# First layer of a two-layer graph network: work of GpSimd moved to VectorE, masks in one-input form, picks at set steps

## The chip, the cores and the metric

The kernel runs on one core of a Trainium2 chip. The core has TensorE (PE in the profile), VectorE (DVE), ScalarE (ACT), GpSimd (POOL) and SyncE (SP), 16 DMA engines, an SBUF of 128 partitions and a PSUM of eight banks. The metric is the device time of one execution in microseconds, lower is better. The kernel before has a median of 3579.48 us over three runs, from 3570.99 to 3601.28.

## The reference

There are 6250 nodes with 128 features, 200,000 edges sorted by destination, eight edge types and four node types.

```python
# first layer
neigh_sum = jax.ops.segment_sum(x[src], dst, num_segments=N)
deg = jax.ops.segment_sum(jnp.ones_like(src, dtype=x.dtype), dst, num_segments=N)
mean = neigh_sum / jnp.maximum(deg, 1.0)[:, None]
neigh_agg = jnp.where(deg[:, None] > 0, mean, x)
h = relu(jnp.concatenate([x, neigh_agg], axis=-1) @ W.T + b)
x1 = layernorm(x + h)
# second layer: attention over the edges
Q, K, V = (type_matmul(x1, W, node_type) for W in (W_Q, W_K, W_V))
k_t = type_matmul(K[src], W_edge, edge_type)
scores = jnp.sum(Q[dst] * k_t, axis=-1) / sqrt(d) * mu[edge_type]
out = segment_sum(V[src] * segment_softmax(scores, dst)[:, None], dst)
y = layernorm(x1 + out)
```

## The kernel before

**Stages.** Setup loads the edges, tests that they are sorted densely enough for the quick form (the other form is a loop that here runs once), and splits x into a bfloat16 part and two rests, x_parts, that sum to it with little loss. The first layer's loop, `l0`, has 49 iterations (ND = TILES = 49). The second layer then works through 98 blocks of 2048 edges and gathers a row of keys and values per edge from `kv_table`.

**The loop of the first layer.** Edges are laid in columns of 128. A period of 32 columns goes through one iteration, in two ways. The first 14 columns, in two halves of HALF = 7, are gathered: GpSimd issues one indirect DMA per column (line 717), which fetches 128 rows of `part_dram` into one of three run buffers `near` (two in the ring, the third over `src_n`). TensorE multiplies each with a mask that says to which node an edge belongs (`belongs`, made by VectorE on line 1414) and sums seven in PSUM: the run product, `run_sum`, line 803, at steps 2 and 23. GpSimd may refill a run buffer once the run product of that buffer is counted in `runs_ps`. The other 18 columns (GCOLS) are done without a gather. For each, VectorE writes two one-hot masks (`hot`, lines 1382 and 1383, six batches of three columns into a ring of nine), TensorE multiplies them (a pick, line 769, into one of two banks), and ScalarE copies the result to SBUF (`take`, line 1138). A pick needs the copy of the pick two before it. With all 18 picks of an iteration copied, the next iteration's 49 slot sums (line 777), one per step h from 0 to 48, multiply them with all of x_parts.

**The tail of a tile** runs inside the same iterations: at iteration i the tile i-2 is `early` (mean, transposes, first product, `relu`, `normalise_x1`) and tile i-3 is `late` (transpose of the normalised rows, `by_types`, key and value projections, `low_keys` and `high_keys`, copies into `kv_rows`). SP stores the rows of x1, the typed rows and the 1 MB table row block of each tile, and loads the next x and types.

**The order is written out by hand.** TensorE's order and its waits are a list of steps h in `l0` of the tensor block: `PICK_AT` gives the steps of the picks, and `HOT_AT`, one step before every third pick, the waits for masks. ScalarE's order is its list of copies c from 0 to 17 with the tile's copies between them. VectorE has its own `l0`: it joins the slot sums of the iteration before, makes masks, adds node sums, does the tile's steps and then stages the keys of the iteration after next (line 1375). In iterations 4 to 12 a digit pass over all 1664 columns comes first (`digit_op`, nine passes; SP stores the result before tile 12). GpSimd's program is the gathers, with two pieces of arithmetic between the first groups: `edge_keys` (three passes over 128x1664, lines 699 to 703) before group 2 and `weights` (eight scalings, line 694) before group 3.

## Time and profile before

| What | Value |
|---|---|
| Median of three runs | 3579.48 us (3570.99 to 3601.28) |
| The profiled execution's own time | 3594.51 us |
| Its span, first to last instruction | 3592.7 us, 38408 instructions |
| Mean granted TensorE clock | 0.839 of full |
| TensorE matmul, busy | 2618.7 us, 73%, 13802 instructions |
| VectorE, busy | 1554.8 us, 43%, 4730 instructions |
| ScalarE, busy | 1151.8 us, 32%, 2057 instructions |
| GpSimd, busy | 2244.9 us, 62%, 2302 instructions |
| Chain that ended last, by engine | GpSimd 36%, TensorE 25%, issue 18%, another core or an unknown queue 13%, VectorE 5% |
| First layer's gathers, line 717 | 462 into the ring at 1028 ns, 224 into src_n at 1038 ns |

The shares are means over both layers, which have different limits. Busy time is from the first to the last record of an instruction; matmuls overlap and their ends are modelled. "Remote" or "another core or an unknown queue" is what the profile says of a wait whose releaser it does not see at that time; this kernel has one core. The granted clock is 1.0 at 2.4 GHz and 0.5 at 1.2 GHz.

### The profile page before, as it was taken

The numbers are of one execution on the slowest core, as the hardware profiler recorded it, in microseconds if no ns is written. First come the engines' busy times: TensorE is split into PE (matmuls) and PEld (weight loads), VectorE is DVE, ScalarE is ACT, GpSimd is POOL, SyncE is SP. The second block draws the span as 40 slices with busy tenths as digits, with TensorE's granted clock in tenths as the row PEclk, the third lists the DMA queues.
The fourth block names the chain that finished last, engine by engine and source line by source line (L and its number), as shares of the span: only waits on it lengthen the run. The fifth ranks groups of instructions, "written<-read, shape, count | busy, mean of one in ns | idle before, by whom it ended". The sixth has DMA issues, their size and how long they took to land.

```text
span 3592.7 us, 38408 instructions
## 1 busy us (share of the span) xinstructions
PE 2618.7 (73%) x13802; PEld 1868.6 (52%) x13802; DVE 1554.8 (43%) x4730; ACT 1151.8 (32%) x2057; POOL 2244.9 (62%) x2302
## 2 busy tenths in 40 slices
PE   3587888887878827777777777777777777777777
PEld 1355566555556625555554555555555555555555
DVE  8476677666667613322322233322322333323223
ACT  4344454444444412222222222222222222222222
POOL 7665566566556454666666666666666666666664
PEclk9799999899999968777778887777777877777778
DMA  6244354444444432333333333333333333333332
GB/s 157 62 129 121 111 144 130 120 126 120 119 119 126 118 122 75 100 99 100 100 100 101 103 100 100 99 97 100 100 100 102 102 100 101 100 99 100 101 100 69
DMA packets 256960, 384.03 MB, mean 107 GB/s; under 512 B 100640, under 2 KB 189003, under 8 KB 250625
## 3 DMA queue, kind: packets, MB, share of 16 engines
q0 software_dynamic: 108112, 273.13, 27.6%
q1 hardware_dynamic: 146833, 107.53, 9.7%
q8 instruction: 108, 1.77, 0.2%
q10 hardware_dynamic: 1824, 0.92, 0.1%
q14 instruction: 83, 0.68, 0.1%
HBM read 304.30 MB, written 77.13 MB: 106 GB/s over the span
## 4 chain that ended last, share of the span: by engine, by line
POOL 36%; PE 25%; issue 18%; another core or an unknown queue 13%; DVE 5%; ACT 2%; DMA 0%; ACTq 0%; DVEq 0%; POOLq 0%
POOL ring L722 35%; PE banks L777 9%; PE banks L769 4%; PE banks L803 3%; PE banks L850 1%; PE banks L862 1%; PE banks L992 1%; PE banks L855 1%; PE banks L1005 1%; ACT picks L1138 1%; PE banks L1029 1%; PE banks L865 1%; PE banks L1021 1%; POOL ring L717 1%
## 5 line engine op out<-in xcount | busy, mean ns | idle before, releaser
L722 POOL DMA_INDIRECT ring<-kv_table,src_n x1563 | 1485.4, 950 | 798.3 <-issue 447.6
L1005 PE MATMUL banks<-identf,ring 128*128 128x128 f32 x1568 | 436.9, 373 | 630.4 <-issue 501.1
L717 POOL DMA_INDIRECT ring<-x_part_rows,work x462 | 475.1, 1028 | 307.4 <-PE banks L803 142.8
L1005 PEld LDWEIGHTS banks<-identf,ring 128*128 128x128 f32 x1568 | 250.9, 182 | 791.1 <-issue 585.2
L777 PE MATMUL banks<-sums,picks 128*126 128x385 bf16 x2401 | 608.1, 342 | 33.3 <-ACT picks L1138 15.3
L1138 ACT ACTIVATE picks<-banks 128x343 bf16<-128x343 f32 x882 | 433.3, 512 | 543.7 <-PE banks L769 333.6
L1227 ACT ACTIVATE work<-banks 128x512 f32<-128x512 f32 x392 | 213.5, 598 | 887.6 <-remote 638.9
L1623 DVE SCALAR_TENSOR_TENSOR sums<-sums,corr,banks 128x128 f32<-128x128 f32 x98 | 34.0, 347 | 1029.2 <-remote 1022.6
L1219 ACT ACTIVATE work<-banks,negmax 128x2048 f32<-128x2048 f32 x98 | 192.8, 1968 | 807.9 <-issue 743.7
L777 PEld LDWEIGHTS banks<-sums,picks 128*126 128x126 bf16 x2401 | 331.6, 143 | 149.4 <-issue 54.1
L769 PE MATMUL banks<-sums 128*128 128x343 bf16 x882 | 286.1, 325 | 168.7 <-issue 105.8
L1604 DVE TENSOR_REDUCE largest<-banks 128x1 f32<-128x2048 f32 x98 | 224.5, 2291 | 370.5 <-PE banks L992 273.6
L1029 PE MATMUL banks<-ring,sums 128*128 128x128 f32 x3136 | 372.7, 277 | 5.6 <-issue 4.5
L992 PE MATMUL banks<-work,queries 128*128 128x512 f32 x784 | 372.8, 619 | 0.0
L1029 PEld LDWEIGHTS banks<-ring,sums 128*128 128x128 f32 x3136 | 358.6, 192 | 6.5 <-issue 5.1
L1661 DVE COPY sums<-banks 128x512 f32<-128x512 f32 x392 | 262.5, 689 | 148.6 <-PE banks L1021 101.7
L717 POOL DMA_INDIRECT src_n<-x_part_rows,work x224 | 232.5, 1038 | 136.6 <-issue 60.5
L1021 PE MATMUL banks<-identf,work 128*128 128x128 f32 x1568 | 313.0, 384 | 1.1 <-ACT work L1219 1.1
L1021 PEld LDWEIGHTS banks<-identf,work 128*128 128x128 f32 x1568 | 303.0, 212 | 2.4 <-ACT work L1219 1.3
L1383 DVE TENSOR_SCALAR sums<-iota_k,keys_g 128x344 bf16<-128x344 bf16 x882 | 288.4, 327 | 0.0
L1382 DVE TENSOR_SCALAR sums<-iota_n,keys_g 128x128 bf16<-128x128 bf16 x882 | 238.7, 271 | 114.3 <-PE banks L769 58.9
L992 PEld LDWEIGHTS banks<-work,queries 128*128 128x128 f32 x784 | 144.7, 195 | 189.7 <-issue 189.7
(260 smaller groups left out, 2363.3 us busy)
## 6 DMA issues: line engine op xcount, KB each, us to landing
kv_table<-ring SPq DMA_DIRECT2D x48, 1024.0 KB
ring<-kv_table,src_n POOLq DMA_INDIRECT x1563
sums<-x_typed SPq DMA_DIRECT2D x99, 128.0 KB
x_typed<-work SPq DMA_DIRECT2D x49, 256.0 KB
ring<-x_part_rows,work POOLq DMA_INDIRECT x462
x_part_rows<-sums SPq DMA_DIRECT2D x7, 675.5 KB, 7.1
src_n<-x_part_rows,work POOLq DMA_INDIRECT x224
sums<-x_rows SPq DMA_DIRECT2D x51, 64.0 KB
```

What stands on the lines that cost most here:

```text
L717: pool.indirect_dma_start(near[k % RUNS][:, j, :], None, part_dram, bass.IndirectOffsetOnAxis(ap=col_ids[:, first + j:first + j + 1], axis ...
L722: pool.indirect_dma_start(kv_ring[u][:, j, :], None, table, bass.IndirectOffsetOnAxis(ap=of, axis=0)).then_inc(l1_rows[2 * u + j // RUN], 16)
L769: pe.matmul(bank[c % 2][:, 0:KEYS], hot_low[:, c % HOT_RING, :], hot_key[:, c % HOT_RING, 0:KEYS], start=True, stop=True).then_inc(pick_ps, 1)
L777: mm = pe.matmul(bank[2 + i % 2][0:SLOTS, 0:3 * D + 1], picked[:, i % 2, h, 0:SLOTS], x_parts[:, h, 0:3 * D + 1], start=(h == 0), stop=(h ...
L992: mm = pe.matmul(bank[g], queries[:, :], keysT[:, g, :], start=False, stop=True, skip_group_check=True)
L1005: tr = pe.transpose(bank[KEY_BANK[g]][:, j * P:(j + 1) * P], kv_ring[k.u][:, g * 4 + j, 0:D], identf[:, :])
L1021: tr = pe.transpose(bank[PROB_BANK[g]][:, j * P:(j + 1) * P], probT[:, at:at + P], identf[:, :])
L1029: mm = pe.matmul(bank[7][:, 0:D], prob[:, j, :], kv_ring[k.u][:, j, D:2 * D], start=(j == 0), stop=(j == COLS - 1))
L1138: act.activation(picked[:, par, :, c * NW:(c + 1) * NW], bank[c % 2][:, 0:KEYS].rearrange("p (h w) -> p h w", w=NW), ACT.Copy).then_inc(pi ...
L1382: dve.tensor_scalar(hot_low[:, c % HOT_RING, :], iota_n[:, :], keys_g[:, par, 1, c:c + 1], None, ALU.is_equal)
L1383: ins = dve.tensor_scalar(hot_key[:, c % HOT_RING, :], iota_k[:, :], keys_g[:, par, 0, c:c + 1], None, ALU.is_equal)
L1661: dve.tensor_copy(prob[:, g * 4:(g + 1) * 4, :].rearrange("p a b -> p (a b)"), bank[PROB_BANK[g]]).then_inc(prob_copied, 1)
```

## The change

GpSimd keeps only its gathers. `weights` and `edge_keys` become VectorE's: the weights in iteration 0, the keys as four pieces of one two-input operation each in iterations 1 and 2. The third run buffer moves from `src_n` to `spare_n`, since `src_n` must live until the keys are made and then serves as the digits' scratch. The digits are made in thirds of the columns, 27 short passes in iterations 4 to 30, no longer ahead of everything; SP's store of them moves from before tile 12 to before tile 30. A run mask is made by seven one-input operations on a bfloat16 `iota_g` rather than by one two-input fp32 operation. `PICK_AT` is a written list, the wait for the first batch of hot masks moves from step 48 to step 2 of the next iteration, and four of ScalarE's copies move by one or two places. VectorE's order within an iteration changes, and the row normalisation of a tile is done at the head of the next iteration.

```diff
-        iota_g = sb("iota_g", [P, P])
+        iota_g = sb("iota_g", [P, P], BF16)
...
-        near_runs = [near_flat[:, 0:HALF * TW // 2], near_flat[:, HALF * TW // 2:], src_n[:, 0:HALF * TW // 2].bitcast(F32)]
+        near_runs = [near_flat[:, 0:HALF * TW // 2], near_flat[:, HALF * TW // 2:], spare_n[:, 0:HALF * TW // 2].bitcast(F32)]
...
+        DIGIT_COLS = [k * CBLKS // 3 * P for k in range(4)]
+        DIGIT_ALL = 3 * DIGIT_OPS
         DIGIT_STEP = 4
+        KEY_OPS = 4
+        KEY_COLS = [k * NAT // KEY_OPS for k in range(KEY_OPS + 1)]
...
-                if t == 12:
-                    sp.wait_ge(digit_vec, DIGIT_OPS)
+                if t == 30:
+                    sp.wait_ge(digit_vec, DIGIT_ALL)
                     store_digits()
...
             for k in range(2 * ND):
-                if k == RUNS - 1:
-                    edge_keys()
-                    pool.wait_ge(keys_nat, 1)
-                if k == RUNS:
-                    weights()
                 if k >= RUNS:
                     pool.wait_ge(runs_ps, k - RUNS + 1)
...
-            PICK_AT = [-(-c * TILES // GCOLS) for c in range(GCOLS)]
+            PICK_AT = [3, 4, 7, 10, 14, 17, 18, 19, 22, 24, 25, 28, 29, 31, 33, 37, 42, 44]
...
-                    if i + 2 < ND and h == TILES - 1:
-                        wait_hot(i + 2, 0)
+                    if 0 < i < ND - 1 and h == 2:
+                        wait_hot(i + 1, 0)
                     slot_sum(i, h)
...
-                    if late and c == 11:
+                    if late and c == 12:
                         copy_high(late)
-                    if early and c == 11:
+                    if early and c == 13:
                         copy_x(early)
-                    if early and c == 13:
+                    if early and c == 14:
                         copy_mean(early)
-                    if early and c == 16:
+                    if early and c == GCOLS - 1:
                         deviation(early)
...
-                dve.tensor_tensor(belongs[h], col_keys[:, 1, first:first + HALF].unsqueeze(2).broadcast_to([P, HALF, P]),
-                                  iota_g[:, :].unsqueeze(1).broadcast_to([P, HALF, P]), ALU.is_equal).then_inc(belongs_ready, 1)
+                for j in range(HALF):
+                    ins = dve.tensor_scalar(belongs[h][:, j, :], iota_g[:, :], col_keys[:, 1, first + j:first + j + 1], None,
+                                            ALU.is_equal)
+                ins.then_inc(belongs_ready, 1)
...
+            def edge_keys(k):
+                at = slice(KEY_COLS[k], KEY_COLS[k + 1])
+                if k == 0:
+                    dve.wait_ge(L["etype"], 48)
+                dve.scalar_tensor_tensor(key_f[:, at], src_n[:, at], float(ET), et_n[:, at], ALU.mult, ALU.add
+                                         ).then_inc(keys_nat, 1)
...
             def l0(i, late, early):
-                if DIGIT_STEP <= i < DIGIT_STEP + DIGIT_OPS:
-                    digit_op(i - DIGIT_STEP)
                 if i > 0:
                     join_parts(i - 1, (i - 1) % 2)
+                if late:
+                    normalise_x1(late)
                 if i + 1 < ND:
                     hot(i + 1, (i + 1) % 2, 2)
-                    belong(i + 1, 0)
                 if i > 0:
                     add_nodes(i - 1)
                 if late:
                     by_types(late)
+                if i + 1 < ND:
+                    hot(i + 1, (i + 1) % 2, 3)
                 if early:
                     mean(early, added(i))
                 if i + 1 < ND:
-                    for q in range(3, BATCHES):
+                    for q in range(4, BATCHES):
                         hot(i + 1, (i + 1) % 2, q)
+                    belong(i + 1, 0)
+                if i == 0:
+                    weights()
+                if 1 <= i <= KEY_OPS // 2:
+                    for k in range(2 * i - 2, 2 * i):
+                        edge_keys(k)
+                if DIGIT_STEP <= i < DIGIT_STEP + DIGIT_ALL:
+                    digit_op(i - DIGIT_STEP)
                 if late:
                     copy_low(late)
                 add_runs(i)
...
-                if early:
+                if i == ND - 1:
                     normalise_x1(early)
```

## Rows read from the trace of the kernel before

**Rows 1.** Windows by stage: length, busy us and count by engine, clock, DMA share, GB/s.

```profile
...
72.60:190.80 118.20, 73.55 (x370) 47.84 (x368) 63.45 (x217) 40.37 (x83) 78.43 (x77) 0.83 0.26 68
190.80:1231.40 1040.60, 861.35 (x4927) 605.79 (x4927) 728.99 (x2860) 483.56 (x1056) 630.91 (x611) 0.94 0.44 124
...
1275.60:3592.70 2317.10, 1633.81 (x8264) 1181.13 (x8264) 680.29 (x1446) 578.11 (x843) 1486.36 (x1564) 0.79 0.35 98
```

**Rows 2.** One line's instructions in the loop: ns, first and last start.

```profile
L1375 DVE COPY keys_g<-work x44: 168/174/179, 187.1 to 1205.3; 128x36 f32<-128x36 f32 x44
```

**Rows 3.** Windows of a fast and a slow iteration, columns as in rows 1.

```profile
498.60:519.70 21.10, 18.55 (x115) 13.24 (x113) 16.63 (x67) 10.86 (x25) 14.72 (x15) 1.00 0.49 139
...
701.70:729.60 27.90, 21.99 (x117) 15.80 (x118) 16.34 (x67) 12.27 (x29) 13.24 (x14) 0.81 0.36 107
```

**Rows 4.** Timeline, fast iteration, TensorE: start, us, count, idle before and releaser.

```profile
511.16 1.32 PE L803 MATMUL banks<-src_n,more_belongs 128*128 128x385 bf16 x7
...
516.68 0.32 PE L769 MATMUL banks<-sums 128*128 128x343 bf16 x1 [1.91 <-issue]
```

**Rows 5.** Timelines of ScalarE, VectorE and GpSimd at the same place.

```profile
516.12 1.42 ACT L1138 ACTIVATE picks<-banks 128x343 bf16<-128x343 f32 x3 [3.31 <-remote]
...
516.18 0.69 DVE L1478 COPY ring<-banks 128x512 f32<-128x512 f32 x1 [2.97 <-remote]
...
513.96 0.95 POOL L717 DMA_INDIRECT ring<-x_part_rows,work  x1 [0.31 <-issue]
516.31 0.95 POOL L717 DMA_INDIRECT src_n<-x_part_rows,work  x1 [1.41 <-remote]
```

**Rows 6.** Waits in the loop: us in total, times, longest.

```profile
ACT picks L1138 <- remote: 144.6, 51, 4.6
```

**Rows 7.** Timelines of VectorE's masks and of the gathers that run beside them.

```profile
497.35 1.09 DVE L1414 TENSOR_TENSOR more_belongs<-work,iota_g 128x896 bf16<-128x896 f32 x1
...
499.29 0.24 DVE L1382 TENSOR_SCALAR sums<-iota_n,keys_g 128x128 bf16<-128x128 bf16 x1
499.44 0.30 DVE L1383 TENSOR_SCALAR sums<-iota_k,keys_g 128x344 bf16<-128x344 bf16 x1
...
505.42 1.09 DVE L1414 TENSOR_TENSOR ring<-work,iota_g 128x896 bf16<-128x896 f32 x1 [0.22 <-remote]
...
497.77 1.49 POOL L717 DMA_INDIRECT ring<-x_part_rows,work  x1 [0.30 <-issue]
499.57 0.99 POOL L717 DMA_INDIRECT ring<-x_part_rows,work  x1 [0.30 <-issue]
...
505.65 1.67 POOL L717 DMA_INDIRECT ring<-x_part_rows,work  x1 [1.32 <-remote]
```

**Rows 8.** Timeline of GpSimd at the start.

```profile
77.53 4.44 POOL L699 TENSOR_SCALAR spare_n<-src_n 128x1664 int32<-128x1664 int32 x1
...
87.73 1.05 POOL L717 DMA_INDIRECT src_n<-x_part_rows,work  x1 [0.28 <-POOL et_n L703]
...
97.06 3.64 POOL L694 TENSOR_SCALAR ring<-ring,mu_b 128x128 f32<-128x128 f32 x8
100.97 1.01 POOL L717 DMA_INDIRECT ring<-x_part_rows,work  x1 [0.27 <-issue]
```

**Rows 9.** Timeline of TensorE at the start: two run products.

```profile
98.71 2.43 PE L803 MATMUL banks<-src_n,ring 128*128 128x385 bf16 x7 [2.87 <-DMA src_n<-x_part_rows,work]
...
111.33 2.18 PE L803 MATMUL banks<-ring,more_belongs 128*128 128x385 bf16 x7 [4.94 <-DMA ring<-x_part_rows,work]
```

**Rows 10.** VectorE groups, 190 to 420 us: busy us, mean ns, idle before.

```profile
L1493 DVE SCALAR_TENSOR_TENSOR digits<-digits 128x1664 bf16<-128x1664 bf16 x1 | 1.9, 1883 | 0.0
```

**Rows 11.** Groups in the loop, shapes kept apart, columns as in rows 10.

```profile
L777 PE MATMUL banks<-sums,picks 128*126 128x385 bf16 x2158 | 547.1, 341 | 26.9 <-ACT picks L1138 13.7 <-issue 10.9 <-DVE ring L1405 2.0
```

**Rows 12.** Timeline of TensorE across an iteration's boundary.

```profile
660.36 0.32 PE L769 MATMUL banks<-sums 128*128 128x343 bf16 x1 [2.23 <-ACT picks L1138]
661.73 0.90 PE L777 MATMUL banks<-sums,picks 128*126 128x385 bf16 x2 [1.04 <-ACT picks L1138]
```

More of the change, by code:

```diff
@@ L689, in _ @@
                                         ).then_inc(gen_loaded, 16)
-            def weights():
-                pool.wait_ge(L["small"], 16)
-                pool.wait_ge(L["weights"], 80)
-                for e in range(ET):
-                    pool.tensor_scalar(we_s[:, e, :], we_s[:, e, :], mu_b[:, e:e + 1], SCALE, ALU.mult, ALU.mult
-                                       ).then_inc(weights_ready, 1)
-            def edge_keys():
-                pool.wait_ge(L["etype"], 48)
-                pool.tensor_scalar(spare_n[:, :], src_n[:, :], float(ET), None, ALU.mult).then_inc(pool_step, 1)
-                pool.wait_ge(pool_step, 2)
-                pool.tensor_tensor(et_n[:, :], spare_n[:, :], et_n[:, :], ALU.add).then_inc(pool_step, 1)
-                pool.wait_ge(pool_step, 3)
-                pool.tensor_copy(key_f, et_n[:, :]).then_inc(keys_nat, 1)
             pool.wait_ge(parts_stored, 16 * (TILES // 7))
@@ L967, in _ @@
             late_part(tile(TILES - 1))
-            pe.wait_ge(keys_nat, 1)
+            pe.wait_ge(keys_nat, KEY_OPS)
             pe.wait_ge(picked_ready, ND * GCOLS + 2)
@@ L1478, in copy_low, with weights, digit_op @@
                 dve.tensor_copy(kv_of(tile)[:, 0:4, 0:D], by_type(bank[6])).then_inc(kw_low, 1)
-            def digit_op(k):
-                dve.wait_ge(*((digit_vec, k) if k else (keys_nat, 1)))
-                X, Y, Z = (digits[:, i, :] for i in range(3))
-                if k == 0:
-                    ins = dve.tensor_scalar(spare_n[:, :], dst_n[:, :], 3, 15, ALU.arith_shift_right, ALU.bitwise_and)
+            def weights():
+                dve.wait_ge(L["small"], 16)
+                dve.wait_ge(L["weights"], 80)
+                for e in range(ET):
+                    dve.tensor_scalar(we_s[:, e, :], we_s[:, e, :], mu_b[:, e:e + 1], SCALE, ALU.mult, ALU.mult
+                                      ).then_inc(weights_ready, 1)
+            def edge_keys(k):
+                at = slice(KEY_COLS[k], KEY_COLS[k + 1])
+                if k == 0:
+                    dve.wait_ge(L["etype"], 48)
+                dve.scalar_tensor_tensor(key_f[:, at], src_n[:, at], float(ET), et_n[:, at], ALU.mult, ALU.add
+                                         ).then_inc(keys_nat, 1)
+            def digit_op(n):
+                dve.wait_ge(*((digit_vec, n) if n else (keys_nat, KEY_OPS)))
+                part, k = divmod(n, DIGIT_OPS)
+                at = slice(DIGIT_COLS[part], DIGIT_COLS[part + 1])
+                X, Y, Z = (digits[:, i, at] for i in range(3))
+                near_dst, spare_d = dst_n[:, at], src_n[:, at]
+                half = half_b[:, at]
+                if k == 0:
+                    ins = dve.tensor_scalar(spare_d, near_dst, 3, 15, ALU.arith_shift_right, ALU.bitwise_and)
                 elif k == 1:
-                    ins = dve.tensor_scalar(X, spare_n[:, :], -2.0, 16.0, ALU.mult, ALU.add)
+                    ins = dve.tensor_scalar(X, spare_d, -2.0, 16.0, ALU.mult, ALU.add)
                 elif k == 2:
-                    ins = dve.tensor_scalar(spare_n[:, :], dst_n[:, :], 7, None, ALU.bitwise_and)
+                    ins = dve.tensor_scalar(spare_d, near_dst, 7, None, ALU.bitwise_and)
                 elif k == 3:
-                    ins = dve.tensor_scalar(Y, spare_n[:, :], -2.0, 8.0, ALU.mult, ALU.add)
+                    ins = dve.tensor_scalar(Y, spare_d, -2.0, 8.0, ALU.mult, ALU.add)
                 elif k == 4:
@@ L1494, in digit_op @@
                 elif k == 5:
[L1495 removed]
+                    ins = dve.scalar_tensor_tensor(half, Y, 0.25, Y, ALU.mult, ALU.mult)
                 elif k == 7:
[L1497 removed]
+                    ins = dve.tensor_scalar(half, near_dst, 0.0, FAR_PLACE, ALU.is_lt, ALU.mult)
                 else:
[L1499 removed]
+                    ins = dve.tensor_tensor(Z, Z, half, ALU.add)
                 ins.then_inc(digit_vec, 1)
             def l0(i, late, early):
[L1503 to L1504 removed]
                 if i > 0:
                     join_parts(i - 1, (i - 1) % 2)
+                if late:
+                    normalise_x1(late)
                 if i + 1 < ND:
                     hot(i + 1, (i + 1) % 2, 2)
[L1509 removed]
                 if i > 0:
```

6 lines of the change are left out of this document (1 added, 5 removed).

## The prediction

> **What bounds the kernel now.** I first cut the span into stages [rows 1]. The second layer is the largest, 2317.1 us from 1275.6 us on. No line of it is edited, and its inputs are the same, so I carry it over unchanged. The first layer's loop runs at a settled pace from 190.8 to 1231.4 us. There TensorE is busy for 861.35 of 1040.6 us, at a mean granted clock of 0.94. Before it lies a start of 118.2 us with TensorE busy for only 73.55. So the change can act on some 1160 us. In the loop the keys are staged once per iteration, 44 times from 187.1 to 1205.3 us [rows 2]: 1018.2 / 43 = 23.7 us an iteration. Two iterations show the ends of the spread [rows 3]: one takes 21.1 us with TensorE busy for 18.55 at full clock, the other 27.9 us at a clock of 0.81.
>
> From these rows the mean iteration splits into three. TensorE's work at full clock is 18.5 us. The clock costs 1.4: at 0.94 with levels of 1.0 and 0.5, 12% of 1040.6 us is spent at 1.2 GHz, 125 us, of which half is lost, 62 us over 44 iterations. TensorE's idle time is (1040.6 - 861.35) / 44 = 4.1 us. Together that is 24.0, close to 23.7.
>
> What sets the 21.1 is the reading that matters most. TensorE's run product at 511.16 us has all its operands and its last matmul ends at 512.5; TensorE goes on, then stops and begins its next pick only at 516.68, 1.91 us idle [rows 4]. In between, ScalarE, VectorE and GpSimd are all waiting for counts that only TensorE raises, and start within 0.2 us of each other: 516.12, 516.18 and 516.31 [rows 5]. GpSimd's last gather of the group of seven before that ended at 513.96 + 0.95 = 514.91. So TensorE's counts arrive about 1.2 us after the gather group in progress ends, although its matmuls were over 3.6 us earlier. I do not know why, but it ties TensorE to GpSimd: the page calls such a releaser "remote", and ScalarE alone lost 144.6 us to it in 51 waits [rows 6]. A cycle of the fast iteration is therefore two gather groups with their gaps: from 505.65 to 516.31 us is 10.66 us, and two such make the 21.1. GpSimd, through this, is the bound of a fast iteration. TensorE is the bound of a slow one, where GpSimd waits for it.
>
> **The change, part by part.**
>
> *Run masks.* Each group's mask is one two-input fp32 operation of 1.09 us. Two gathers that begin beside one take 1.49 and 1.67 us, while one beside the one-input hot masks takes 0.99, and one beside nothing 0.95 [rows 7, 5]. Two masks per iteration so cost GpSimd 0.54 + 0.72 = 1.26 us of the 21.1. The new form is seven one-input masks of the shape of the hot mask on line 1382. Two such masks start 0.15 us apart or a little more [rows 7], so seven are about 1.1 us and VectorE's time stays as it is. Upper bound: seven at 0.25, 1.75 us, also hidden, since VectorE is busy for 16.6 of 21.1 us [rows 3]. What they do to a gather lies between nothing and the old 1.26; nearest is the row beside hot masks, +0.04 per gather, so some 0.15 us per iteration comes back. Gain 1.1 us in an iteration bound by GpSimd, nothing in the others. By the two ends of rows 3, the mean of 23.7 makes (27.9 - 23.7) / 6.8, 60%, fast ones; I take half, 22. **-24 us**, bounds 0 and -48.
> The Trainium skill ("SBUF — State Buffer", section "SBUF: two separate sides") says that VectorE and GpSimd share a port pair as an exclusive lock, which a 2-port fast mode takes always and a two-input operation only against a GpSimd operation that reads SBUF. By that rule the new masks, in a fast mode, would block as the old ones do, and the sum would be 24 us worse. The trace shows the two-input form hurting and the fast form (0.04 us) hardly at all.
>
> *GpSimd's own arithmetic.* Edge keys held its gathers from 77.53 to 87.73, 10.2 us, the weights from 97.06 to 100.97, 3.9 us [rows 8]. TensorE then waited 2.87 and 4.94 us for two gathered groups [rows 9]. Gain: at least those 7.8, at most all 14.1 us. I take **-10**, as the waits on held counts that follow are not removed. What moves to VectorE: eight weight scalings, which cost GpSimd 3.64 us and so VectorE hardly more; four key pieces (one pass rather than three, each over a quarter of the columns); all in iterations 0 to 2, where VectorE is busy for 63.45 of 118.2 us [rows 1]. That idle time covers them. Without it, some 6 us: 3.64 and about one pass of 1.88 [rows 10]. The third run buffer moves to another tile, which costs nothing. The digit stores stay on SP's queue but go behind tile 30 rather than 12: six issues that wait for nothing by then, needed first after the loop.
>
> *Digits in thirds.* Nine passes of 1.0 to 1.9 us (the largest row 1.88 [rows 10]) stood ahead of everything in VectorE's iterations 4 to 12, so ahead of masks TensorE needs. Now 27 passes of a third stand behind the masks. Between nothing and nine times 1.9, 17 us; near the middle, **-8**. The added fixed costs, 18 instructions of about 0.1 us, are hidden on VectorE.
>
> *Picks by time.* The last pick was at step 47 of 49, and TensorE's first slot sum of the next iteration waits for ScalarE's copy of it. The idle time before slot sums is 26.9 us in the loop [rows 11]; now the last pick is at step 44, and this goes. The wait for the first hot masks of the iteration after next, at step 48, moves to step 2 of the next; an iteration boundary shows 2.23 us before a pick and 1.04 before the slot sum [rows 12]. If ten boundaries have the 2.23, that is 22 more. In a fast iteration the held counts take the time back, so half: **-25**, bounds 0 and -49. Against it: the picks after the second run product now stand at steps 24, 25 and 28, not 25, 28 and 30. A pick needs the copy of the one two before it, and that copy waits for the held count, so TensorE stops two steps earlier. A step is one matmul, at most 0.19 us by the seven in 1.32 [rows 4]: at most 0.38 x 44 = +17, and at least 0. I take **+5**, as in a fast iteration GpSimd sets the pace.
>
> *Deferred normalisation* takes VectorE's wait for ScalarE's square root off the end of an iteration. It puts the row normalisation behind the join of the slot sums, still ahead of step 9 where TensorE transposes it. SP's store and reload of x wait for it about 1 us longer, with nobody waiting for them. Node sums and row types now come ahead of the run mask: the old mask waited for the run product just before them. Both: 0, bounds +-5.
>
> *The clock.* If TensorE idles less it falls to 1.2 GHz less often; of the 62 us I take a tenth, **-6**, bounds +20 and -30.
>
> Sum: -24 - 10 - 8 - 25 + 5 - 6 = -68 us against the profiled execution's 3594.5, so 3526.5. That execution lay 15.0 us above the median of 3579.5, so the forecast is **3511 us**.
>
> **The rivals.**
>
> *Hidden anyway (0.22).* TensorE's held counts and its clock set the pace whatever the masks do; the mean of 23.7 against the fast 21.1 speaks for it, the 1.49 and 1.67 against. Only the start and the digits count: 3579.5 - 10 = about 3569.
>
> *The masks still lock GpSimd (0.13).* The seven fast masks follow each other without a gap, other than the pairs in rows 7, and the gather beside them is blocked for all of their 1.1 us. The 24 us stay away: 3535. This is the skill's lock rule as a mechanism of this kernel.
>
> *Picks run into the held counts (0.12), slower.* The place is steps 3 to 7 and 24 to 28. The first pick now stands right behind the first run product, and the pick at step 7 needs its copy. Between that run product and step 7 lie five slot sums, two picks (0.19 each, 1.3 us) and four small node products, some 1.8 us; if the count is held longer than this, TensorE stops there too, about 0.5 us, and 0.3 at step 28. With the idle time the clock falls more often, so some 1.0 us for 44 iterations is +44, and less 10 for the start: about 3615. For it: each hold lasts 3.6 us in rows 4. Against it: with shorter gather groups holds end sooner.
>
> *All iterations become fast (0.08).* At 21.1 - 1.1 = 20.0 us each, 44 take 880 of 1040.6 us: -160, and -10: 3409, with the clock's share perhaps 3430.
>
> **How the numbers follow.** The forecast has 0.45, the likeliest case, and 3511 is its time. The range takes in the forecast's bounds as far as they are not all on one side, the case of locked masks, and the hidden case with its spread: 3435 to 3578. What it leaves out is the slower rival and most of the fast one, under 0.2. About 1% (36 us) is what a measurement can tell from no change. Faster by more: 0.45 + 0.13 + 0.08 = 0.66; within: 0.22; slower: 0.12.
>
> **What would show it.** Masks: gathers beside the new masks take about 1.0 us and none 1.5; the fast iterations last 20.0. Start: no GpSimd arithmetic, and the run products at 98.71 and 111.33 come 3 and 8 us earlier. Picks: the idle time before slot sums falls from 26.9 us to near 5. Digits: iterations 4 to 12 no longer than the rest. The forecast is wrong if the staging of keys still comes every 23.7 us, or if TensorE's idle time of 179 us only moves to the picks at steps 7 and 28; if the second layer moves by over 10 us, the cause lies outside my steps.

## The result and the profile after

The changed kernel has a median of 3607.85 us (3595.10 to 3623.57, eight runs), the kernel before, timed beside it, 3574.06 us (3551.95 to 3601.28, eight runs). The ratio is 1.0084 with an interval of 1.0045 to 1.0124. All ratios here leave out the slow runs of either kernel (over 1.5% above its fastest, among them single ones of 6683 and 4587 us). I had forecast 3511 us; the change makes the kernel slower by a little. The profiled execution took 3607.77 us, with a span of 3606.0.

Three words are used from here on. A count is the increment of a semaphore that TensorE makes when a matmul ends and for which another engine waits. A count is held when it is recorded well after the end of its matmul. A group is the seven gathers that fill one run buffer.

The stages come first, in windows with the columns of [rows 1]: the loop (from the first slot sum of iteration 4 to that of iteration 48), and the rest.

```profile
186.80:1242.30 1055.50, 846.08 (x4929) 585.48 (x4930) 745.09 (x3410) 472.03 (x1056) 593.41 (x609) 0.98 0.43 122
1242.30:3606.00 2363.70, 1671.47 (x8451) 1212.07 (x8450) 703.97 (x1530) 590.06 (x869) 1500.37 (x1566) 0.78 0.35 99
```

In the kernel before the loop is 190.8 to 1231.4 [rows 1], and the rest:

```profile
1231.40:3592.70 2361.30, 1666.77 (x8450) 1205.35 (x8450) 701.95 (x1528) 589.57 (x868) 1487.50 (x1566) 0.79 0.35 99
```

The 13.3 us between the spans are -4.0 in the start, +14.9 in the loop and +2.4 behind it. The -4.0 is no gain that can be told from chance: e9 and e10 below run the changed kernel's program up to iteration 24, and their start ends at 187.5 and 173.9 us. In the loop GpSimd's busy time falls from 630.91 us [rows 1] to 593.41, as forecast: no gather of 609 takes over 1.3 us, where it was 63 of 611. TensorE's clock rises from 0.94 to 0.98. Yet an iteration takes 24.0 us and not 23.65, for TensorE's idle time grew by 30.2 us (1055.50 - 846.08 = 209.4, before 179.2) and its busy time fell by only 15.3. Where it idles, by line and by waits in the loop:

```profile
L760 PE MATMUL banks<-sums,picks 128*126 128x385 bf16 x2157 | 545.6, 331 | 73.2 <-ACT picks L1121 71.5 <-issue 1.7
```

```profile
ACT picks L1121 <- remote: 231.6, 72, 5.1
POOL ring L700 <- PE banks L786: 193.0, 57, 5.7
...
POOL spare_n L700 <- PE banks L786: 91.4, 26, 5.4
```

The idle time before slot sums, which was to fall from 26.9 [rows 11] to near 5 us, is 73.2. ScalarE's waits for held counts ("remote") went from 144.6 us [rows 6] to 231.6. GpSimd waits 284.4 us for run products; the same two rows of the kernel before add to 184.0:

```profile
POOL ring L717 <- PE banks L803: 124.5, 29, 9.8
...
POOL src_n L717 <- PE banks L803: 59.5, 15, 10.0
```

Timelines of one turn show the pattern, TensorE, GpSimd and ScalarE:

```profile
506.06 0.32 PE L752 MATMUL banks<-sums 128*128 128x343 bf16 x1 [2.49 <-issue]
507.58 2.42 PE L786 MATMUL banks<-spare_n,more_belongs 128*128 128x385 bf16 x7
```

```profile
497.55 0.95 POOL L700 DMA_INDIRECT ring<-x_part_rows,work  x1 [3.98 <-PE banks L786]
...
505.17 0.96 POOL L700 DMA_INDIRECT ring<-x_part_rows,work  x1 [0.30 <-issue]
510.27 1.24 POOL L700 DMA_INDIRECT spare_n<-x_part_rows,work  x1 [4.14 <-PE banks L786]
```

```profile
505.39 0.61 ACT L1121 ACTIVATE picks<-banks 128x343 bf16<-128x343 f32 x1 [4.32 <-remote]
```

The group of gathers ends at 506.13. ScalarE has waited 4.32 us for the count of a pick made long before, TensorE stops 2.49 us for ScalarE's copy, and only then, behind the pick, comes the run product at 507.58 that lets GpSimd go on, 4.14 us idle. In the fast iteration of before, the stop at 516.68 stood behind the run product at 511.16 [rows 4], and GpSimd lost 1.41 us [rows 5]. The clock has fallen as well: the granted clock is 1.00 from 500 to 506 us and 0.53 from 507.5 to 510, so this product takes 2.42 us and not 1.32. In the changed loop TensorE stops at the pick of step 19 for 74.7 us in 39 iterations, and at the slot sum of step 0 for 73.2 us in 41: both ahead of a run product (steps 23 and 2).

### The profile page after: what moved, and what is told of

The parts are those of the page before. It is cut to its first block, busy times and chain, and to the rows that moved or that the text cites. A ratio compares the mean times of both kernels' runs of the same rounds, so it can differ in the third digit from the quotient of the medians.

```text
span 3606.0 us, 39015 instructions
## 1 busy us (share of the span) xinstructions
PE 2609.4 (72%) x13802; PEld 1853.7 (51%) x13802; DVE 1569.0 (44%) x5348; ACT 1138.9 (32%) x2057; POOL 2207.2 (61%) x2291
## 4 chain that ended last, share of the span: by engine, by line
POOL 40%; PE 25%; issue 17%; another core or an unknown queue 13%; ACT 4%; DVE 2%; DMA 0%; ACTq 0%; DVEq 0%; POOLq 0%
POOL ring L705 40%; PE banks L760 9%; PE banks L752 6%; ACT picks L1121 2%; PE banks L786 2%; PE banks L833 1%; PE banks L845 1%; PE banks L838 1%; PE banks L848 1%; ACT ring L1143 1%; PE banks L775 1%; PE banks L975 1%; PE banks L805 0%; PE banks L1004 0%
## 5 line engine op out<-in xcount | busy, mean ns | idle before, releaser
L988 PE MATMUL banks<-identf,ring 128*128 128x128 f32 x1568 | 414.7, 367 | 632.8 <-issue 400.0
L700 POOL DMA_INDIRECT ring<-x_part_rows,work x462 | 451.8, 978 | 342.0 <-PE banks L786 209.4
L975 PE MATMUL banks<-work,queries 128*128 128x512 f32 x784 | 387.6, 640 | 0.0
L700 POOL DMA_INDIRECT spare_n<-x_part_rows,work x224 | 218.0, 973 | 163.2 <-PE banks L786 99.3
L1365 DVE TENSOR_SCALAR sums<-iota_n,keys_g 128x128 bf16<-128x128 bf16 x882 | 230.7, 262 | 193.8 <-remote 106.9
L1366 DVE TENSOR_SCALAR sums<-iota_k,keys_g 128x344 bf16<-128x344 bf16 x882 | 280.6, 318 | 0.1
```

What stands on the lines that cost most here:

```text
L700: pool.indirect_dma_start(near[k % RUNS][:, j, :], None, part_dram, bass.IndirectOffsetOnAxis(ap=col_ids[:, first + j:first + j + 1], axis ...
L975: mm = pe.matmul(bank[g], queries[:, :], keysT[:, g, :], start=False, stop=True, skip_group_check=True)
L988: tr = pe.transpose(bank[KEY_BANK[g]][:, j * P:(j + 1) * P], kv_ring[k.u][:, g * 4 + j, 0:D], identf[:, :])
L1365: dve.tensor_scalar(hot_low[:, c % HOT_RING, :], iota_n[:, :], keys_g[:, par, 1, c:c + 1], None, ALU.is_equal)
L1366: ins = dve.tensor_scalar(hot_key[:, c % HOT_RING, :], iota_k[:, :], keys_g[:, par, 0, c:c + 1], None, ALU.is_equal)
```

## The experiments

The table takes each loop from the same two slot sums: us per iteration, TensorE's idle time in the 44 iterations, its mean clock, and held counts: those of TensorE's counts in the loop that arrive over 0.8 us after their matmul's end, of all that the records let me match. Of the 1320 that a loop raises 15 to 31% have no record or no match, and with another way of matching the first two rows are 221 of 1073 and 266 of 1038 and the two brakes 13 and 5: the column tells some 250 from some 20, no more.

The runs came in series, each with the kernel before timed beside it, and ratios are against that. Its medians were 3644 us (e1 to e4), 3646 (e5 to e8), 3570 (e9 to e12), 3013 (e13 to e16) and 3579 (e17, e18). The other columns come from one profiled execution each, and the first two rows' from the first series of all (3574 us). They carry the difference between series with them: the rest behind the loop, the same work in every kernel, takes 2361 to 2364 us in the first two profiles and 2376 to 2382 in those of e1 to e8. So compare a ratio with a ratio, and across series with caution.

| Kernel | ratio, interval | iteration | idle | clock | held |
|---|---|---|---|---|---|
| before | 1 | 23.65 | 179 | 0.94 | 250 of 1126 |
| changed | 1.0084 (1.0045-1.0124) | 23.99 | 209 | 0.98 | 312 of 1072 |
| e1 changed, old picks | 1.0386 (1.0284-1.0488) | 27.19 | 259 | 0.88 | 243 of 977 |
| e2 before, new picks | 0.9886 (0.9827-0.9945) | 23.35 | 170 | 0.98 | 274 of 1005 |
| e3 changed, old masks | 1.0151 (1.0024-1.0277) | 24.96 | 214 | 0.92 | 239 of 1032 |
| e4 before, new masks | 1.0459 (1.0355-1.0564) | 27.85 | 282 | 0.87 | 237 of 937 |
| e5 before, both | 1.0339 (1.0292-1.0386) | 27.24 | 291 | 0.93 | 281 of 908 |
| e6 e2 and start, digits | 0.9895 (0.9823-0.9968) | 23.93 | 182 | 0.95 | 258 of 997 |
| e8 products earlier | 1.0132 (1.0076-1.0188) | 25.42 | 223 | 0.90 | 275 of 991 |
| e11 changed, brake | 1.0200 (1.0144-1.0257) | 25.16 | 224 | 0.91 | 22 of 1019 |
| e12 e5, brake | 1.0236 (1.0164-1.0308) | 25.37 | 232 | 0.91 | 7 of 1036 |
| e17 e4, memset | 1.0413 (1.0371-1.0454) | 26.45 | 246 | 0.90 | 260 of 1009 |
| e18 changed, memset | 1.0053 (1.0025-1.0080) | 23.76 | 204 | 0.98 | 309 of 1082 |

**e1 and e2: the picks.** The edit, in e2 forwards and in e1 back:

```diff
-            PICK_AT = [-(-c * TILES // GCOLS) for c in range(GCOLS)]
+            PICK_AT = [3, 4, 7, 10, 14, 17, 18, 19, 22, 24, 25, 28, 29, 31, 33, 37, 42, 44]
```

with the wait for hot masks and ScalarE's order of copies.

> The changed kernel with the pick steps, the wait for the first hot masks and ScalarE's copy order of the kernel before; all the rest of the change stays. Held-count theory: TensorE's counts raised late in a gather group arrive 1.0 to 1.5 us after the group's end. In the changed kernel the pick at step 19 and the slot sum at step 0 stand before the next run product and wait for such a count, so groups and products take turns: 24.0 us an iteration. With the old steps the stalled picks stand behind the run products again, and with the shorter groups an iteration falls to 20 to 22 us: 80 to 150 us faster than the changed kernel, below the kernel before. Rival, VectorE's order: the deferred normalisation and the late run masks make TensorE wait; then the time stays within 15 us of the changed kernel's 3608.

> The kernel before with the changed kernel's pick steps, wait for the first hot masks and ScalarE copy order alone. Held-count theory: the pattern of the changed kernel appears: idle time at steps 19 and 0, few falls of the clock, and with the longer groups (9.1 to 9.3 us rather than 8.8) an iteration of 24.3 to 24.8 us, so 25 to 50 us slower than the kernel before, with the start unchanged. Rival, VectorE's order: the time stays at the kernel before's 3574 within 15 us or falls, since only VectorE's order cost time.

The held-count theory is flatly wrong in both: without the new picks the changed kernel is 3% slower still, and alone they make the kernel before 1.1% faster. e2's rival, which puts the loss on VectorE's order, had the time right. The loss is not in the picks.

**e3 and e4: the run masks.**

```diff
-                dve.tensor_tensor(belongs[h], ...broadcast_to([P, HALF, P]), ALU.is_equal).then_inc(belongs_ready, 1)
+                for j in range(HALF):
+                    ins = dve.tensor_scalar(belongs[h][:, j, :], iota_g[:, :], col_keys[...], None, ALU.is_equal)
+                ins.then_inc(belongs_ready, 1)
```

> The changed kernel with the run mask as one two-input fp32 operation again, on the same places. Held-count theory: in the changed kernel GpSimd's group lies on the cycle twice per iteration, so the masks' lock of GpSimd costs its 0.5 to 0.7 us wherever the mask runs beside a gather: up to 1.2 us an iteration, 20 to 50 us slower than the changed kernel. Rival, the masks do not matter: within 10 us of it; if the masks in one-input form are themselves the loss, faster than it.

> The kernel before with the one-input run masks alone. Held-count theory and my forecast's term: gathers lose their 1.49 and 1.67 us cases, groups take 8.6 us rather than 9.1 to 9.3, the fast iterations go from 21.1 to 20.0 us, and the time falls by 24 to 48 us. Rival, the clock takes it back: TensorE's margin in a fast iteration shrinks, falls to 1.2 GHz become as frequent or more, and the time stays within 10 us.

e3 does not show the gain that taking the masks out should have brought if they alone were the loss: 1.0151 beside 1.0084, with intervals that overlap. In the changed kernel the new masks cost nothing that can be told. In the kernel before they do: alone they make it 4.6% slower where e4's expectation was 24 to 48 us faster, though the median gather is 0.95 us and one of 609 takes over 1.3. Waits of e4's loop, then its timelines of TensorE and GpSimd:

```profile
PE banks L769 <- ACT picks L1138: 187.9, 89, 4.4
...
PE banks L777 <- DVE ring L1405: 0.4, 1, 0.4
```

```profile
POOL ring L717 <- PE banks L803: 324.9, 58, 6.9
POOL src_n L717 <- PE banks L803: 137.5, 25, 6.9
```

```profile
704.33 0.32 PE L769 MATMUL banks<-sums 128*128 128x343 bf16 x1 [2.93 <-issue]
...
704.65 2.22 PE L803 MATMUL banks<-ring,more_belongs 128*128 128x385 bf16 x7
```

```profile
707.14 0.94 POOL L717 DMA_INDIRECT ring<-x_part_rows,work  x1 [3.66 <-PE banks L803]
```

TensorE stops at the pick of step 22 (146.5 us in 41 iterations), which stands ahead of the run product of step 23. The granted clock is 1.00 from 700 to 704.3 us and 0.56 from 704.6 to 707, so the product takes 2.22 us instead of 1.32 [rows 4], and GpSimd waits for all of it, 462.4 us in the loop where it was 184.0. Shorter groups became longer waits for the next. It is not VectorE's time: 0.4 us of TensorE's idle time in this loop ends with VectorE, 223 us with ScalarE's copies.

**e5 and e6: together, and the rest.**

> Before with the one-input run masks, and with the new places of the picks (and their wait for hot masks and ScalarE's order of copies). Alone the masks made before 4.6% slower and the picks made it 1.1% faster. If the two are independent it comes out 3.5% above before. Theory of the phase (what the short gather groups cost is decided by whether a held pick stands just ahead of a run product; the picks' places decide that): the masks' loss mostly goes away, within 1% of before, iterations of 23.5 to 24 us. Rival (the masks cost VectorE or GpSimd time of their own whatever the picks do): 2.5% or more above before, iterations of 26 us.

> Before with the new picks, and with the start and digits of the change: GpSimd only gathers, VectorE scales the weights and makes the edge keys, digits in thirds at the head of VectorE's iterations. Two-input run masks and VectorE's other order as before. If these parts are worth what I forecast (10 us at the start, 8 for the digits), it lies 0.5% below before with new picks alone, so 1.6% below before. Rival, where the loss between that kernel and the changed one with old masks (2.6%) comes from these parts: 1% or more above before, and then VectorE's order and the deferred normalisation are innocent; if it stays at -1.1 to -1.6%, the loss is in VectorE's order or the deferral.

The masks cost 4.6% with the new picks too (1.0339 / 0.9886), so with VectorE's old order the two are independent, and e5's theory of the phase is wrong. The start and the digits are worth nothing (0.9895 against 0.9886). What is left of the change is VectorE's order and the deferred normalisation. It makes the kernel 2.6% slower with the old masks (e6 to e3) and 2.5% faster with the new ones (e5 to changed). It has no price of its own. Both steps compare across series. Inside one series, with the start and the digits taken in, it is 2.7% slower by the ratios from e2 to e3 (1.9% by the means of their runs) and 0.7% faster from e4 to e1, both of these with the new masks (3788 to 3801 and 3765 to 3773 us). So the loss beside the old masks is firm, and the gain beside the new ones is there, but its size is not.

**e7: no gathers** in iterations 25 to 48.

```diff
-                for j in range(HALF):
+                for j in range(HALF if k < 50 else 0):
```

> The changed kernel, with the gathers of its groups 50 to 97 left out (iterations 25 to 48): the run products of those iterations take stale rows at once. GpSimd only passes its waits there. One trace shows the loop with and without gathers. Theory (TensorE's counts are held because GpSimd is issuing gathers): from iteration 25 on no count lags by over 0.1 us, TensorE's idle time at picks and slot sums goes, the clock stays at full speed, and an iteration takes 18.5 to 20 us against 24 before it. Rival (the held counts are TensorE's own affair, or that of its clock or of ScalarE and VectorE): lags and stalls stay, an iteration takes 22.5 us or more.

Its windows, one inside the part with gathers and one without:

```profile
184.40:666.00 481.60, 377.57 (x2028) 258.90 (x2029) 311.88 (x1423) 194.26 (x433) 246.33 (x253) 0.90 0.38 109
730.00:1142.00 412.00, 412.00 (x2593) 309.98 (x2591) 372.16 (x1781) 248.05 (x556) 0.00 (x0) 1.00 0.26 90
```

Without them each iteration takes 17.8 us (26.5 with them in this run, iterations 4 to 23), TensorE is never idle and no count is held. The holds come with the gathers, and both together cost 8.7 us an iteration here. The 26.5 is a warning too: up to iteration 24 this is the changed kernel, whose own profile has 23.9 us in the same iterations, so against that the cost is 6.1 us. e7, e9 and e10 are one execution each.

**e8: run products at steps 0 and 17.**

```diff
-            RUN_AT = (2, 23)
+            RUN_AT = (0, 17)
```

> The changed kernel with its run products moved ahead of the two places where TensorE stalls most: from steps 2 and 23 to steps 0 and 17, each before the pick and the slot sum of that step (the waits for run sums and masks move to step 48 and 16). The stalls stood at the pick of step 19 (74.7 us) and the slot sum of step 0 (73.2 us), and GpSimd idled 3.7 to 4.1 us ahead of each group for the product behind them. Theory of the phase: GpSimd starts its groups earlier and works while TensorE is stalled instead of after it, so its idle time before a group falls by 2 us or more and an iteration goes from 24.0 to 22.5 us or less: 60 us, 1.7% faster than the changed kernel. Rival (a group of gathers holds the counts wherever it lies, so an earlier group only stalls the picks elsewhere): within 0.7% of the changed kernel, with the stalls at other steps.

Wrong again: an iteration takes 25.4 us, not 22.5 or less. TensorE:

```profile
707.56 1.32 PE L786 MATMUL banks<-ring,more_belongs 128*128 128x385 bf16 x7
...
713.85 0.32 PE L752 MATMUL banks<-sums 128*128 128x343 bf16 x1 [3.47 <-ACT picks L1119]
```

The product's own count is held too, 4.3 us, and comes at 713.13, 0.16 us after the last gather of the group in progress has landed (GpSimd starts its next at 713.39), and the uneven halves of 17 and 32 steps leave GpSimd idle in the long one. Its waits for run products are 286.3 us in this loop, no less than the 284.4 of the changed kernel.

**e9 and e10: bytes.** Half rows, and a second 1 MB store per tile, from iteration 25 on.

```diff
+                    wide = TW if k < 50 else TW // 2
```

```diff
+                if tile.t >= 24:
+                    sp.dma_start(twin[...], kv_rows...).then_inc(row_stored, 16)
```

> The changed kernel; its groups 50 to 97 (iterations 25 to 48) gather half of each row, from other places, so as many gathers and rows with half the bytes, and their run products take wrong values. Reading behind it: a count that TensorE raises is held in 9 of 10 cases when two or more gathers are issued and have not landed, in 1 of 100 when none is, and is let go within 0.2 us of a gather's landing; a gather is issued every 1.25 us and lands 1.3 to 3 us after its issue ends. Theory of the backlog (the transfers, not GpSimd's issuing, make the hold): with half the bytes gathers land sooner, two are seldom in flight, the held counts become rare, and an iteration goes from 24.0 us to 18.5 to 21. Rival (GpSimd's writing of descriptors makes the hold, whatever they move): iterations stay at 23.5 us or more.

> The changed kernel; from iteration 25 on the store of the key-value rows, 1 MB on SP's queue, is made twice, the extra one to a spare tensor ahead of the other. The store's packets fill the 16 DMA engines for some 3 us (share 0.97) and the gathers beside it land 1 to 2 us late. Theory of the backlog: the extra 3 us of full engines hold one more gather or two, so an iteration goes from 24.0 to 26 us or more, with more counts held beside the store. Rival (the hold has to do with GpSimd alone, SP's transfers are innocent): iterations stay within 0.5 us of those before iteration 25.

e9's iterations stay at 23.8 us with half the bytes (24.4 in the iterations with whole rows), as its rival said. Its premise did not hold either: half the bytes shorten the median time from a gather's issue to its landing only from 1.49 to 1.27 us. So the size of the rows hardly matters, and how many gathers are in flight was not varied. e10's iterations go from 24.1 to 24.8, between its two forecasts. A backlog of bytes is not what makes the holds; a backlog of gathers stays open.

**e11 and e12: a brake.** Before each gather GpSimd waits for the landing of the gather two before (g below), so that no more than two are in flight.

```diff
+                    g = k * HALF + j - 2
+                    if g >= 0:
+                        pool.wait_ge((run_rows, run_odd)[b % 2][u], ...)
```

> The changed kernel; GpSimd begins a gather only when the one two before it has landed (odd and even gathers of a group count on semaphores of their own). Work and bytes are the same. Theory of the backlog: where a backlog would form GpSimd waits instead, so at most two gathers are in flight, holds get shorter, and the kernel is 1 to 3% faster than the changed one, iterations 21.5 to 23 us. Rivals: the added waits only lengthen the groups (14 gathers of 1.25 us already fill 17.6 of 24 us), within 0.7% or slower; or one gather in flight is enough for a hold, and nothing changes.

> Before with one-input masks and new picks (3.4% slower than before, iterations of 27.2 us) with the same brake on GpSimd. The old masks lengthened two gathers of a group to 1.49 and 1.67 us; if that was a brake that kept a backlog from forming, a wait for the landing does the same: 1.5 to 4% faster than without it, so within 2% of before. Rival (the masks hurt by their place in VectorE's order, not by what they no longer do to the gathers): 3% or more slower than before, as without the brake.

The held counts all but vanish, 22 and 7 in place of 312 and 281. But the gathers come too slowly, and TensorE now waits for their rows: 221 of its 224 us of idle time in e11, 227 of 232 in e12. e11 is 1.2% slower than the changed kernel where 1 to 3% faster was expected; e12 is 1.0% faster than e5, less than the 1.5 to 4% expected. TensorE and GpSimd in e12:

```profile
703.84 2.43 PE L810 MATMUL banks<-src_n,ring 128*128 128x385 bf16 x7 [4.95 <-DMA src_n<-x_part_rows,work]
```

```profile
706.44 0.95 POOL L723 DMA_INDIRECT ring<-x_part_rows,work  x1 [0.72 <-DMA ring<-x_part_rows,work]
```

With holds gone, 1.020 and 1.024 overlap, where the same two kernels stood at 1.008 and 1.034. That speaks for a difference in how the changed kernel and e5 meet the holds, and not in their work. It is not proof, as both now wait for rows, which can hide other differences.

**e13 to e18: the length of a group.** e13 (and e17, the same kernel) is e4, and e15 (and e18) is the changed kernel, each with one memset (0.35 us) behind the fourth gather of each group. e14 and e16 are milder brakes on e2 (three back; two back, for the last three gathers only).

```diff
+                    if j == 3:
+                        pool.memset(pad_tile[:, :], 0.0).then_inc(padded, 1)
```

> Before with the one-input masks (4.6% slower than before, iterations of 27.85 us), and GpSimd does one memset of 128x256 behind the fourth gather of each group, which gives a group some 0.4 us of the 0.6 us back that the two-input masks cost it. Theory of the phase (with shorter groups TensorE's stalls stand ahead of the run products, so that a group and TensorE's work alternate; a group of the old length restores the old phase): within 2% of before, iterations of 24.5 us or less. Rival (the loss comes from the masks on VectorE or from something else than the groups' length): 3.5% above before or more.

> Before with the new picks (1.1% faster than before), and GpSimd begins a gather only when the one three before it has landed. With a brake at two, held counts went from about 300 to 7 or 22 in the loop, but TensorE then waited for late rows. If a hold needs a third gather begun while two have not landed, this brake leaves the holds as they are (some 270) and the time within 0.7% of the kernel without it. If it needs four, holds go at hardly any price, and the kernel is 2 to 4% faster than before.

> The changed kernel (0.8% slower than before) with the same memset in each gather group. Theory of the phase: groups of the old length bring TensorE's stalls behind the run products again, 0.5% or more faster than the changed kernel, so as fast as before or faster. Rival (the pause is only time lost, 0.9 us in each iteration that GpSimd bounds): 0 to 1% slower than the changed kernel.

> Before with the new picks, and the brake at two only for the fifth to the seventh gather of a group. Holds began 4 to 6 us into a group, so at the fourth or fifth gather. If the backlog that makes them grows over the group, the late brake removes most holds (under 100 left) for some 0.6 us a group, and the kernel is 1 to 2% faster than with new picks alone. Rival (each saved hold is paid back as a wait for rows at the run product, as with the full brake): within 1% of it, or slower, with TensorE's idle time at steps 2 and 23.

These four ran in a series in which the kernel before took 3011.0 to 3014.6 us, and no count was held in any of them (none of 1313 that can be matched in e15). The loop of e15:

```profile
144.00:947.00 803.00, 793.53 (x4930) 584.63 (x4929) 753.69 (x3410) 472.38 (x1056) 627.40 (x706) 1.00 0.57 161
```

Its iterations take 18.25 us, near what 14 gathers and two memsets take back to back (14 x (0.97 + 0.30) + 2 x 0.35 = 18.5). Ratios there: e13 1.0107 (1.0090-1.0124), e14 1.0292 (1.0274-1.0309), e15 0.9966 (0.9951-0.9980), e16 1.0326 (1.0308-1.0344). With nothing held, a brake can only lose: TensorE waits 71 us for rows in e14's loop and 88 in e16's. How much of the 2.9 and 3.3% that is can't be said, since e2 without a brake was not timed in this series. For the question they were made for they say nothing, so two ran again:

> The kernel of e13 once more, for a chip that holds TensorE's counts (there the same kernel without the memset was 4.6% slower than before, with 237 held counts and iterations of 27.85 us). Theory of the phase: within 2% of before, iterations of 24.5 us or less. Rival (the groups' length is not what matters): 3.5% above before or more. If the kernel before takes some 3013 us again, no count is held and the run repeats e13: 1% above before.

> The kernel of e15 once more: the changed kernel (0.8% slower than before where counts are held) with the memset in each gather group. Theory of the phase: as fast as before or faster. Rival: 0 to 1% slower than the changed kernel, so 0.8 to 1.8% above before. On a chip without held counts it repeats e15: 0.3% faster than before.

e17 stays at 4.1% above before: giving back 0.35 of the 0.5 us that the new masks take off a group (7 gathers, mean 1.03 and 0.96 us) does not undo the masks' loss. e18 is at 1.0053 against the changed kernel's 1.0084, intervals overlapping, and not as fast as before. The theory that the group's length alone sets the phase is not borne out.

## Why the prediction was wrong

**GpSimd as the bound: the step that failed.** From [rows 4, 5] I made GpSimd "the bound of a fast iteration" and priced its time one to one: run masks -24 us, bounds 0 and -48, "nothing in the others". The gathers did become shorter as written (none over 1.3 us, 37.5 us less of them in the loop), but the time did not come back: GpSimd's waits for run products rose by 100.4 us, from 184.0 to 284.4, and TensorE's idle time by 30.2. As a part of its own the masks' worth had the wrong sign: +4.6% alone, +4.6% with the new picks, and nothing that can be told in the changed kernel (e3). The bound excluded a loss without a reason. Counts of TensorE are held while gathers are under way. TensorE stops at another step than before, and where the stop lies ahead of a run product GpSimd pays it again. GpSimd was one of two partners that wait for each other.

**VectorE's order and the deferred normalisation: 0, bounds +-5, the second step.** I gave them nothing because I saw nobody wait for them. With the old masks beside them they cost 2.6%, some 90 us: e3, which has no new masks, is 1.5% slower than before. With the new masks they give time back. The two were not taken apart. As the parts don't add, the +34 us measured can't be shared out among them: adding picks, start and digits, VectorE's order and masks in this order gives about -1.1, 0, +2.6 and -0.7%, and with the masks second it is -1.1, +4.6 and -2.5% for the rest.

**Masks still lock GpSimd.** Refuted: seven masks on line 1398 take 1.2 to 1.5 us, the gathers beside them 0.95 to 1.24, with the same median (0.96) as the others. By the lock rule of the Trainium skill ("SBUF — State Buffer", section "SBUF: two separate sides") the fast masks should have blocked as the old ones did, if they run in a 2-port mode, which no trace here tells; the measured gathers show no such block.

**GpSimd's own arithmetic, -10, and digits, -8.** Together nothing measurable (e6 against e2). The third and fourth run products, forecast 3 and 8 us earlier than 98.71 and 111.33 [rows 9], came at 109.82 and 126.40. Where the arithmetic had kept GpSimd from gathering, it now gathers without a pause, and ScalarE gets no count from TensorE until 89.74 us. TensorE's next pick then comes after a stop of 6.75 us:

```profile
90.25 0.47 PE L752 MATMUL banks<-sums 128*128 128x343 bf16 x1 [6.75 <-ACT picks L1121]
```

I had named the waits on held counts and not priced them.

**Picks by time, -25 and +5.** Right in sign, and larger than the -20 forecast: e2 measured 1.1%, some 40 us, e1 2.9%. The mechanism is only in part the named one. The ten stops at the boundary's pick were there (21.6 us in 10 times) and are gone. But the idle time before slot sums was to go, and in e2 it grew, 41.5 us at step 0 where before had 24.1, and step 19 has 30.5. TensorE's idle time fell from 179 to 170 us in all, so that the size comes out near is luck.

**Picks run into the held counts**, the slower rival, gave 3615 us, near the 3608 measured, but for another reason: its place was steps 7 and 28, and taking the new picks out makes the kernel slower. **Hidden anyway** (3569) had the right spirit, and its error is the sign. It also says that start and digits count and takes off the start's 10 alone; with both it is about 3561.

**The clock, -6.** It rose from 0.94 to 0.98, TensorE's busy time fell by 15.3 us, and idle time took its place and more. That TensorE "idles less" was not the reason: it idled more.

**Open:** why the one-input masks put TensorE's stop ahead of the run product, and why they do no harm in VectorE's new order. That the stop stands there is shown; that the group's length does it is not; their place and their seven instructions on VectorE were not varied alone. The versions that are fastest where counts are held are e2 and e6, 1.1% and 1.0% below before.

## What to carry over

Where engines wait for each other through held counts, parts of a change have no prices that add: the same part was worth -2.5% and +2.6%. So is a kernel with one part added or left out no price list: e4 alone would have blamed the masks for 4.6%, e3 acquits them. Before an engine's time is priced one to one, look whether it is also idle for the partner (GpSimd lost 184 us to run products before the change), and give a "gain" in such a loop a bound on the other side. Take the resource away altogether in half of the iterations, as e7 did, to see what the coupling costs.

## What the hardware showed

A count that TensorE raised arrived late when gathers were in flight, that is begun and not landed (a landing is the last of the 16 packets of 4 bytes that end a gather). In the changed kernel's loop none of the 103 counts raised with no gather in flight came over 0.5 us late, 17% of 280 with one, 28% of 541 with two, 87% of 111 with three. Of those held over 0.8 us 56% arrived within 0.2 us of a gather's landing, where 23% would by chance. A held count does not wait for the group's end: the one in the timeline above comes at 505.37 us, with the group's last gather begun at 505.17 and landed at 507.44.

The number in flight is not the whole cause. With three, the kernel before has 37% of 174 late and not 87%. With two, the changed kernel has 28% late and e11, under the brake, 13 counts of 788. And in the series of e13 to e16 three or more were in flight for 23% of e15's loop (14% in the changed kernel's) and nothing was held, with the kernel before 16% faster than in the other series (3013 against 3570 to 3646 us). So gathers are needed for a hold and are not enough.

That series differs in more than held counts of TensorE. The part behind the loop takes 2030 to 2051 us in its profiles and 2360 to 2382 in all others. Of the 10976 counts that the first layer's gathers raise when they land, e15's trace has a record of 10793, the changed kernel's of 3166. So the disturbance takes in the counts of transfers too, or at least their records; what it is stays open. It is not a fixed property of one chip: the record names the same chip, number 13, for e13 to e16 and for e17 and e18, where counts were held again.
